# Two transformer layers on one core: the first layer's order of work rebuilt

## The reference

```
def _L0_attn_ref(x, Wq, Wk, Wv, Wo):           # no heads, attention over channels
    q = x @ Wq;  k = x @ Wk;  v = x @ Wv
    scores = einsum('bes,bfs->bef', q^T, k^T) / sqrt(8)     # 256 x 256
    return (softmax(scores) @ v^T)^T @ Wo
def _L0_ffn_ref(h):                             # inner width 1024
    gate, up = split(h @ w_gate_up^T);  return (silu(gate) * up) @ w_down^T
x = x + _L0_attn_ref(_layernorm(x), ...)
x = x + _L0_ffn_ref(_layernorm(x), ...)
x = x + _L1_attn_ref(_layernorm(x), ...)        # 32 heads of 64, 8 key/value heads, rotary, causal
x = x + _L1_ffn_ref(_layernorm(x), ...)         # ternary weights, absmax quantised activations, gelu
```

## Time and profile before

| | us |
|---|---|
| three runs | 668.40, 668.41, 666.92 (median 668.40) |
| the profiled execution | 665.93 |
| its span, first to last instruction | 664.1 |
| TensorE busy | 581.0 (87%) |
| VectorE busy | 464.1 (70%) |
| ACT busy | 435.5 (66%) |
| GpSimd busy | 458.4 (69%) |

### The profile page before, as it was taken

How to read it: one execution, slowest core, us unless ns; L and a number is a source line. 1 busy time by engine, 2 the same in 40 slices (tenths; PEclk the granted TensorE clock), 3 DMA queues, 4 the chain that set the end, 5 groups by cost and what they waited for, 6 DMA issues and landing times.

```text
span 664.1 us, 16866 instructions
## 1 busy us (share of the span) xinstructions
PE 581.0 (87%) x7134; PEld 490.3 (74%) x7134; DVE 464.1 (70%) x762; ACT 435.5 (66%) x599; POOL 458.4 (69%) x404
## 2 busy tenths in 40 slices
PE   3888979797888989999999999999999977965796
PEld 2776868786666878888878788888888866854475
DVE  5384556576767877887777777787787765627796
ACT  2232411124889879789788887877987987821694
POOL 7023244442899998998999799799899868742221
PEclk9998989898999999999999999999999999977799
DMA  9050000400699999999999999999999999990001
GB/s 302 16 180 10 0 1 21 83 1 21 108 179 197 193 183 190 196 183 190 181 201 181 201 188 189 192 187 185 198 180 180 182 193 197 195 177 0 1 25 40
DMA packets 317195, 91.79 MB, mean 138 GB/s; under 512 B 305984, under 2 KB 316224, under 8 KB 317120
## 3 DMA queue, kind: packets, MB, share of 16 engines
q1 hardware_dynamic: 316032, 89.67, 77.2%
q10 hardware_dynamic: 1088, 1.05, 0.5%
HBM read 13.11 MB, written 1.05 MB: 21 GB/s over the span
## 4 chain that ended last, share of the span: by engine, by line
PE 38%; DMA 19%; POOL 18%; DVE 11%; ACT 7%; issue 5%; SPq 1%; POOLq 0%; ACTq 0%; DVEq 0%
PE PS L1118 23%; DMA pT_lo<-p_lo 18%; POOL p_lo L487 12%; PE PS L1350 6%; PE PS L1367 4%; DVE small L972 2%; POOL roped L476 2%; ACT p_hi L662 2%; ACT probs L653 2%; PE PS L1371 1%; POOL roped L473 1%; SPq L372 1%; POOL moments L438 1%; DMA pT_hi<-p_hi 1%; DVE stats L748 1%
## 5 line engine op out<-in xcount | busy, mean ns | idle before, releaser
L487 POOL TENSOR_TENSOR p_lo<-probs,p_hi 128x1280 f16<-128x1280 f32 (+7 forms) x128 | 303.8, 2392 | 38.8 <-DMA pT_lo<-p_lo 29.2
L653 ACT ACTIVATE probs<-PS,small 128x640 f32<-128x640 f32 (+7 forms) x256 | 173.7, 742 | 46.1 <-DVE small L972 40.1
L972 DVE TENSOR_REDUCE small<-PS 128x2 f32<-128x1280 f32 (+7 forms) x128 | 172.9, 1351 | 28.7 <-PE PS L1350 27.1
L662 ACT CAST p_hi<-probs 128x1280 f16<-128x1280 f32 (+7 forms) x128 | 145.3, 1159 | 6.9 <-DMA pT_hi<-p_hi 6.1
L1350 PE MATMUL PS<-k_hi,q_hi 64*128 64x512 f32 (+2 forms) x384 | 75.3, 386 | 13.6 <-ACT probs L653 11.0
L1367 PE MATMUL PS<-v_hi,pT_hi 128*128 128x65 f16 x1152 | 79.1, 195 | 1.1 <-DMA pT_hi<-p_hi 0.7
L1371 PE MATMUL PS<-v_lo,pT_hi 128*128 128x64 f16 x1152 | 78.9, 195 | 0.0
L1350 PE MATMUL PS<-k_lo,q_hi 64*128 64x512 f32 (+2 forms) x384 | 78.4, 402 | 0.0
L1367 PEld LDWEIGHTS PS<-v_hi,pT_hi 128*128 128x128 f16 x1152 | 73.6, 99 | 5.0 <-issue 2.8
L1371 PEld LDWEIGHTS PS<-v_lo,pT_hi 128*128 128x128 f16 x1152 | 72.7, 98 | 0.4
L1350 PE MATMUL PS<-k_hi,q_lo 64*128 64x512 f32 (+2 forms) x384 | 67.7, 346 | 0.0
(11 more groups left out here) (190 smaller groups left out, 1431.3 us busy)
## 6 DMA issues: line engine op xcount, KB each, us to landing
wgu_nat<-L_ffn_w_gate_up SPq DMA_DIRECT2D x2, 1024.0 KB, 10.8
wkq_nat<-L_attn_wq SPq DMA_DIRECT2D x8, 256.0 KB, 3.4
wo_nat<-L_attn_wo SPq DMA_DIRECT2D x8, 256.0 KB, 3.3
x<-L_attn_x SPq DMA_DIRECT2D x4, 256.0 KB, 5.3
wdn_nat<-L_ffn_w_down SPq DMA_DIRECT2D x1, 1024.0 KB, 13.1
wfc_nat<-L_ffn_w_fc SPq DMA_DIRECT2D x1, 1024.0 KB, 5.7
wpj_nat<-L_ffn_w_proj SPq DMA_DIRECT2D x1, 1024.0 KB, 8.1
pT_hi<-p_hi SPq DMA_TRANSPOSE x64, 5.8
```

What stands on the lines that cost most here:

```text
L487: nc.gpsimd.tensor_tensor(p16_lo[G % 2][:, cols], probs[G % 2][:, cols], p16_hi[G % 2][:, cols], ALU.subtract).then_inc(p_lo_done, 1)
L653: nc.scalar.activation(probs[G % 2][:, start:start + w], PS[:, src:src + w], ACT.Exp, bias=nmax[:, 4 * (G % 2) + u:4 * (G % 2) + u + 1]).t ...
L662: nc.scalar.copy(p16_hi[G % 2][:, cols], probs[G % 2][:, cols]).then_inc(p_hi_done, 1)
L972: nc.vector.tensor_reduce(nmax[:, first:first + 2], both_heads(part)[:, :, 0:blocks(G, part) * P], AX.X, ALU.max, negate=True).then_inc(nm ...
```

## The change

Six edits, all before the second layer:

1. The Gram matrix is accumulated tile by tile in two PSUM banks, each tile as soon as it is normalised, and the transposes of the tokens come after it: the first half directly, the second half behind the `Wq` product. `Wv` is transposed behind the `Wk` product.
2. The statistics of both first-layer normalisations are made for pairs of tiles (one add and one power over two columns, `rstd_pair`), and the pairs of the first are ahead of GpSimd's masks. The four attention weights are loaded from SP's queue behind x, no longer from ACT's.
3. The transposes of `w_down` (k = 8 to 11) and their copies move into the gate-up loop, behind n = 3 to 6.
4. Gate-up starts when the first half of the tokens is mixed, normalised and transposed; the second half's adds, normalisations and transposes lie beside gate-up 0 and 1. Gate-up takes the high parts first, and waits for each chunk. A SiLU on one column is put ahead of it on ACT.
5. `wv`'s maximum over the partitions: VectorE multiplies the identity by the column of row maxima (`wv_diag`), TensorE multiplies `ones` by it behind gate-up 8, VectorE takes the maximum of the row.
6. The down products wait for `hT_lo` inner tile by inner tile, no longer for all eight.

The core of the diff:

```diff
@@ SP
+            for j, (w, dst) in enumerate(((wk_a, wk_a_sb), (wq_a, wq_a_sb), (wv_a, wv_a_sb), (wo_a, wo_a_sb))):
+                sp.dma_start(dst[:], rows(w)).then_inc(wa_landed[j], 16)
@@ GpSimd
+            def rstd_pair(st, j, eps):
+                v = moments[:, st, 4 * j + 1:4 * j + 4:2]
+                pool.wait_ge(moments_done, st * NT + 2 * j + 2)
+                nc.gpsimd.tensor_scalar(v, v, eps, None, ALU.add).then_inc(var_eps_done, 1)
+                pool.wait_ge(var_eps_done, 4 * st + j + 1)
+                nc.gpsimd.tensor_tensor(v, v, neg_half.broadcast_to([P, 2]), ALU.pow).then_inc(rstd_done, 1)
...
-                if n == 5:
-                    pool.wait_ge(wv_max_done, 1)
-                    nc.gpsimd.partition_all_reduce(wv_all, wv_max, P, bass.bass_isa.ReduceOp.max)\
-                      .then_inc(wv_all_done, 1)
@@ ACT
             for n in range(2 * NF):
...
+                if n == 1:
+                    for c in range(KC):
+                        x_high(1, 1, c, 6 + c)
+                if 3 <= n < 7:
+                    w_high(5 + n)
@@ VectorE
             for i in range(NT):
-                dve.wait_ge(x_landed[i // 2], 16)
+                if i % 2 == 0:
+                    dve.wait_ge(x_landed[i // 2], 16)
                 tile_moments(0, i)
-                if i:
-                    normalise(0, i - 1)
+                if i % 2 and i > 1:
+                    normalise(0, i - 3)
+                    normalise(0, i - 2)
...
                 if n == 3:
...
+                    dve.wait_ge(wv_max_done, 1)
+                    nc.vector.tensor_scalar(wv_diag[:], identf[:], wv_max, None, ALU.mult).then_inc(wv_diag_done, 1)
                 if n == 8:
+                    dve.wait_ge(wv_spread_done, 1)
+                    nc.vector.tensor_reduce(wv_all, bank(5)[:, 0:P], AX.X, ALU.max).then_inc(wv_all_done, 1)
@@ TensorE
+            for i in range(NT):
+                pe.wait_ge(xn_done, i + 1)
+                for m in range(KC):
+                    last = nc.tensor.matmul(bank(m)[:, 0:C], xn[:, i, m * P:(m + 1) * P], xn[:, i, :], start=i == 0,
+                                            stop=i == NT - 1)
...
-            for hf in range(2):
-                x_transposes(0, hf, 4)
-
-            for m in range(KC):
-                product(bank(m)[:, 0:C], [(xn[:, i, m * P:(m + 1) * P], xn[:, i, :]) for i in range(NT)])\
-                    .then_inc(chain_pe, 1)
...
             def gate_up(n):
-                if ft == 0:
-                    pe.wait_ge(xT_lo_done, 4 + 2 * hf + 2)
...
-                if n == 0:
-                    pe.wait_ge(x_added, 4)
+                if n < 2:
+                    pe.wait_ge(x_added, 2 * n + 2)
...
+                    for c in range(KC):
+                        if ft == 0 and half == 0:
+                            pe.wait_ge(xT_hi_done, 4 + 2 * hf + c + 1)
+                        nc.tensor.matmul(dst, wguT_hi[:, c, ft_s], xnT_hi[:, c, tok], start=c == 0, stop=False)
+                        nc.tensor.matmul(dst, wguT_lo[:, c, ft_s], xnT_hi[:, c, tok], start=False, stop=False)
+                    for c in range(KC):
+                        if ft == 0 and half == 0:
+                            pe.wait_ge(xT_lo_done, 4 + 2 * hf + c + 1)
+                        last = nc.tensor.matmul(dst, wguT_hi[:, c, ft_s], xnT_lo[:, c, tok], start=False,
+                                                stop=c == KC - 1)
...
             def down(j):
-                pe.wait_ge(h_lo_done, NF * (hf + 1))
...
+                    for i in range(NF):
+                        if t % 4 == 0:
+                            pe.wait_ge(h_lo_done, hf * NF + i + 1)
...
+                if n == 1:
+                    x_transposes(1, 1, 4)
+                if 3 <= n < 7:
+                    w_transposes(5 + n)
                 if n == 8:
+                    pe.wait_ge(wT_lo_done, 12)
...
+                    pe.wait_ge(wv_diag_done, 1)
+                    nc.tensor.matmul(bank(5)[:, 0:P], ones[:], wv_diag[:], start=True, stop=True)\
+                      .then_inc(wv_spread_done, 1)
```

## The result

| | before | after |
|---|---|---|
| median of the runs, us | 667.66 (666.22 to 668.41, 4 runs) | 642.69 (642.03 to 643.39, 4 runs) |
| profiled execution, its span | 665.93, 664.1 | 642.03, 640.2 |
| TensorE, VectorE, ACT, GpSimd busy | 581.0, 464.1, 435.5, 458.4 | 573.9, 462.9, 436.1, 453.3 |

The ratio of the times is 0.9629, with a 95% interval of 0.9606 to 0.9651. The forecast was 645.0, with cases from 640 to 652 around it.

A forecast was written before the change was run, and what follows sets the result against it. TensorE, busy 581.0 of 664.1 us, was taken to bound the kernel before the attention loop. Terms -8.8 - 7.9 + 3.2 - 5.8 - 4.2 = -23.5 us gave 642.4 profiled, 645.0 from the median; cases 640 to 652.

The forecast's parts named there:

- First term: Program start to mixing: Gram matrix runs from 7.3 to 15.7 us, mixing starts at 30.1; 8.8 us saved.
- rival of a fast start: Gram product: TensorE at the fast pace from its first product, Gram ends 1.5 us earlier, 643.5 us; chance 0.08.
- Second term: Mixing to the end of gate-up 0: 11.4 us instead of 19.3, normalising by halves; 7.9 us saved.
- rival of a fall to 1.2 GHz: Between mixing and gate-up 0: TensorE's clock falls, gate-up 0 nearly doubles, +2 us, 647 us; chance 0.10.
- Third term: Gate-up: the x and wdn transposes and the wv_diag product now stand between its steps; 3.2 us added.
- Fourth term: Before the first down product: TensorE's 4.37 us wait and 1.4 us of slow clock go; 5.8 us saved.
- rival that its "issue" might be another's: GpSimd before the first down product: its stall stays or returns as another wait, 650.8 us; chance 0.08.
- Fifth term: Third down product: waiting by tiles leaves 0.9 us of a 3.4 us wait and avoids the low clock; 4.2 us saved.

The follow-up runs named there:

- e5: Changed kernel with the four attention weight loads issued from ACT's queue again, beside the x loads; median 644.64 us, ratio 0.9654.
- e4: Changed kernel plus nine identity products on TensorE before the first tile comes; median 643.35 us, ratio 0.9632.
- e7: Changed kernel with the whole second normalisation, all 1024 tokens, done before gate-up 0 again; median 650.68 us, ratio 0.9747.
- e9: Kernel before with only the maximum of wv made by a product on TensorE instead of GpSimd's partition reduction; median 663.19 us, ratio 0.9934.
- e8: Changed kernel with the transposes and copies of w_down put back ahead of mixing; median 643.68 us, ratio 0.9637.
- e10: Kernel before with only the down products' tile-by-tile waits for hT_lo, partition reduction kept on GpSimd; median 661.05 us, ratio 0.9891.
- e1: Changed kernel with the partition maximum of wv put back on GpSimd as a reduction; median 645.49 us, ratio 0.9679.
- e2: Changed kernel with the down products waiting for all eight inner tiles at their start again; median 650.02 us, ratio 0.9741.
- e12: Changed kernel plus nine early identity products and 16 identity transposes filling TensorE's rest before the first scores; median 643.03 us, ratio 0.9621.
- e3: Changed kernel with the Gram product waiting for all eight normalised tiles before its first matmul; median 648.59 us, ratio 0.9721.

## Why the prediction was right, step by step

- **First term, -8.8; measured -9.25.** The stages came as forecast (Gram from 7.3 to 15.7; it was 6.37 to 15.48), but by two misses that cancel, which is luck. I costed the moved loads at nothing; without other loads beside them the x loads start VectorE 1.03 us earlier, and with the loads back on ACT's queue (e5) it starts 1.14 later. The slow start took 9.11 us for the product where I took 8.4. From there to mixing it was 14.11, where I had 14.4. The operation on two columns took as long as I assumed (1.05 us for both parts; 1.08 assumed). That the first products run slowly beside a clock column of 1.00 was read rightly from the durations. The rival of a fast start did not come; even with nine products ahead (e4) only 1.07 us of its 1.5 were gained.
- **Second term, -7.9; measured -7.69.** The second half of the tokens is covered as said. The fourth add ends at 39.94 where I had 40.4. The rival of a fall to 1.2 GHz did not come, but my ground against it was a misreading. I took the 1.00 in 48:49 for a level that outlasts such a rest; one microsecond later, from 50 us, the same trace has 0.50, up to and into gate-up 0. The clock stayed up because halving the normalisation divides the rest (0.77 and 0.33 us are left of it), and not because it holds over a long one, so on this point the forecast had luck: with the whole normalisation ahead of gate-up 0 (e7) the clock was 0.68 in the window before it, and mixing to the copy took 4.6 us more. The stage came out right as I built it up from single steps at the upper level and subtracted a measured time that had the fall in it.
- **Third term, +3.2; measured +3.13.** The product with `wv_diag` took 0.47 us where I took 0.3 in bounds of 0.12 and 0.5, but it added only 0.25 to its stage in e9. The transposes of `wdn` are only moved (1.94 by e8), those of x too (0.93 by e7); the three make 3.12.
- **Fourth term, -5.8; measured -5.91,** and by e9, this edit alone, -5.92. Both parts, 4.37 of wait and 1.4 of clock, hold. What the prediction left out is that the waits by tiles overlap with it: alone they take 2.95 us of the same stretch (e10). I wrote that the first two down products gain nothing from them. That holds only once the reduction is gone. The sum is right since both edits are made; a sum of the parts measured each alone (5.92 and 7.04) would be about 3 us too large.
- **The stall belongs to the reduction.** The rival that its "issue" might be another's is refuted: it comes back with the instruction (e1, 13.1 us around 0.38) and is gone without it (e9). Why so short an instruction holds the engine so long stays open. The Trainium skill, "GPSIMD Engine Reference", section "4.1 Engine selection", gives reductions along partitions to GpSimd. Here the stall around the instruction's own 0.38 us decides against that rule. The product on TensorE, the multiplication and the reduction on VectorE take 0.47, 0.29 and 0.28 us.
- **Fifth term, -4.2; measured -4.07,** and e2 gives 4.04. The one wait was forecast at 0.9 and is 0.81; the upper clock level held over it (1.00 in 101.30:105.00). My ground for that was again the window 48:49 of the earlier trace rows, which does not carry it, since the level fell one microsecond later; so far as it rested on that window, this was luck.
- **What was not in the sum:** -1.6 at the entry of the loop and +2.2 in the tail, each with a clock difference beside it, and -0.7 in the loop, in this pair of executions. Their sum is small, -0.1, and that they cancel is luck. The first comes and goes between kernels whose edits do not touch it (40.1 to 40.6 or 39.0); the tail took 74.3 to 75.8 in all other kernels, so that the 72.5 of the execution before is the odd one, for which I have no cause.
- **From trace to time:** the profiled execution was forecast at 642.4 and took 642.03. I added 2.5 us to get from it to a median, 645.0. The median of the kernel after is 642.69, 0.7 above its profiled execution. This step, not one of the terms, makes most of the 2.3 us of error: how far a profiled execution stood from the median did not carry over from the kernel before to the one after. With its fourth run the kernel before has a median of 667.66 instead of 668.40, so between the medians the change is 25.0 us.

## What to carry to other kernels

Read what an instruction costs its engine from the gap around it, not from its own duration, and move it if a neighbour can do the same in three short steps. Let a consumer wait for each of its inputs in the order in which it uses them: that removes a wait at the end, and here it also hid half or more of a stall elsewhere. Gains that cover the same wait can't be added, so such edits must be tested each alone. A rest of TensorE of 2.3 to 4.4 us cost its own length and, where the clock fell, 1.2 to 1.6 us more in the pace behind it (the old first down product, e2, the entry of the loop), so dividing a rest can be worth something even if its sum stays; e10 and gate-up 0 point that way. And read the clock over the whole of a rest and of what follows it: one window at 1.00 inside it proves nothing.

## What the runs showed of the hardware

- One partition reduction of 0.38 us held GpSimd for 13.1 to 13.9 us in three kernels (before, e1, e10): about 5.7 us ahead of it and 7 to 8 behind it. Two `MODIFY_POOL_CONFIG` of its line stand where each stall begins.
- At the start of the program TensorE's passes took 634 ns while the granted clock read 1.00. How many did so varied: in the first 3 us of the Gram product of the kernel before they were most of eight, in e9, the same up to there, less than half of eleven. The same 32 passes took 8.64 to 10.22 us over the nine kernels with the changed start and nothing of TensorE's ahead of them, and 7.64 and 7.98 behind the nine products of e12 and e4. The Trainium skill, "TensorE: Matmul & The Clock Gate", section "Part 1: The HAM clock gate", calls the slow start variable from run to run; these durations, of one execution each, are in line with that.
- Four weight loads on another engine's queue delayed VectorE's first x tile by about 1 us: 4.59 to 4.78 us in the four kernels with them there, 3.47 to 4.27 in the other ten.
- After the same rest of 2.30 us the first 2 us of scores had a clock of 1.00 in two kernels (after, e3) and of 0.56 to 0.86 in ten. With 0.55 us of rest left it was 1.00 both times.
- Gate-up 0 began at a fallen clock in all four kernels with the whole normalisation ahead of it (before, e7, e9, e10; 4.0 to 5.4 us to the first SiLU), and at 1.00 in all ten others (3.1 us in after).
- A gain of 1.8 us at the entry of a loop of 421 us had shrunk to 1.0 at its exit (e12 against e4). Over the fourteen kernels the loop took 420.5 to 423.8 us with the same instructions.
